# Attention: upper-half value matmuls four steps earlier, query projections five to six steps later

## The reference

```python
q = (x @ Wq).reshape(b, n, 16, 64).transpose(0, 2, 1, 3) * scale
kv = concat([null_kv, x @ Wkv], axis=1)            # 1025 keys, one head of 64, shared
sim = einsum('bhid,bjd->bhij', q, kv)              # masked above the diagonal
attn = softmax(sim)
out = einsum('bhij,bjd->bhid', attn, kv)           # keys are also the values
return out.transpose(0, 2, 1, 3).reshape(b, n, 1024) @ Wout
```

## Time and profile before

| | |
|---|---|
| median of 3 runs | 1478.52 us (1477.1 to 1479.38) |
| the profiled execution | 1478.79 us, span 1477.1 us |
| attention, first score tile of pair 0 to that of pair 15 | 450.70 to 1006.75 us of the span |
| TensorE / VectorE / ScalarE / GpSimd busy over the span | 86% / 77% / 62% / 23% |
| mean granted TensorE clock | 0.956 |
| DMA engines | 59 GB/s mean, 24.9% of their time |

### The profile page before, as it was taken

The page is one execution under the profiler, slowest core; times in us unless marked ns, Lnnn a source line. Parts: engine busy times, 40 slices in busy tenths (PEclk is TensorE's granted clock), DMA queues, the critical chain, the costliest instruction groups (busy, mean ns, idle before and its releaser), DMA issues. The chain is left out here.

```text
span 1477.1 us, 28019 instructions
## 1 busy us (share of the span) xinstructions
PE 1271.0 (86%) x8305; PEld 535.3 (36%) x8368; DVE 1136.6 (77%) x1941; ACT 919.3 (62%) x1915; POOL 332.7 (23%) x552
## 2 busy tenths in 40 slices
PE   3699999999757999999989999999967999999985
PEld 2122222222234555555556555555641222222222
DVE  6889999999856666676644666666649999999996
ACT  3288888888726555555533555555334888888884
POOL 4200000001003334333422333343331000000200
PEclk9599999999969999999999999999976999999999
DMA  4512112452122222222220222220043211135412
GB/s 126 167 42 59 53 52 65 76 94 62 30 53 45 46 46 45 44 44 45 45 45 6 49 50 49 49 56 12 1 128 98 59 49 51 48 79 87 83 44 58
DMA packets 58909, 86.49 MB, mean 59 GB/s; under 512 B 22288, under 2 KB 32464, under 8 KB 58832
## 3 DMA queue, kind: packets, MB, share of 16 engines
q1 hardware_dynamic: 58832, 85.53, 24.9%
HBM read 37.79 MB, written 22.54 MB: 41 GB/s over the span
## 5 line engine op out<-in xcount | busy, mean ns | idle before, releaser
L916 DVE TENSOR_REDUCE neg_max<-ps 128x1 f32<-128x1024 f32 x512 | 601.5, 1218 | 53.2 <-PE ps L1157 44.0
L771 ACT ACTIVATE arena<-ps 128x512 f32<-128x512 f32 x1024 | 538.8, 603 | 150.3 <-PE ps L1172 147.5
L1172 PE MATMUL ps<-arena 50*128 50x512 bf16 x1024 | 311.1, 388 | 59.8 <-ACT arena L771 41.4
L992 DVE TENSOR_REDUCE a_neg_max<-ps 128x1 f32<-128x129 f32 (+7 forms) x256 | 193.2, 755 | 168.7 <-PE ps L1274 165.3
L1157 PE MATMUL ps<-arena 48*128 48x512 bf16 x1024 | 269.2, 397 | 18.9 <-DVE neg_max L916 16.9
L1186 PE MATMUL ps<-arena 128*32 128x512 f32 x2048 | 275.5, 611 | 3.3
L578 POOL TENSOR_SCALAR arena<-arena,a_rsum 128x128 f32<-128x128 f32 (+7 forms) x256 | 191.3, 747 | 376.8 <-DVE a_rsum L1000 365.7
L1274 PE MATMUL ps<-arena 128*128 128x512 bf16 (+4 forms) x1281 | 227.8, 301 | 15.2 <-ACT null_out L722 4.8
L685 ACT ACTIVATE arena<-ps,a_neg_max 128x129 f32<-128x129 f32 (+7 forms) x256 | 189.5, 741 | 60.7 <-DVE a_neg_max L992 58.5
L1172 PEld LDWEIGHTS ps<-arena 50*128 50x128 bf16 x1024 | 77.5, 94 | 413.2 <-ACT arena L771 370.8
L695 ACT ACTIVATE arena<-ps 128x128 f32<-128x128 f32 (+1 forms) x192 | 87.0, 453 | 206.6 <-PE ps L1287 205.3
(11 more groups left out here) (120 smaller groups left out, 804.5 us busy)
## 6 DMA issues: line engine op xcount, KB each, us to landing
arena<-stack_dram SPq DMA_DIRECT2D x128, 192.0 KB, 3.4
stack_dram<-arena SPq DMA_DIRECT2D x48, 256.0 KB, 3.7
arena<-arena SPq DMA_DIRECT2D x32, 384.0 KB, 4.4
o_dram<-arena SPq DMA_DIRECT2D x32, 256.0 KB, 2.1
arena<-arena SPq DMA_DIRECT2D x32, 256.0 KB, 5.0
arena<-o_dram SPq DMA_DIRECT2D x30, 256.0 KB, 4.4
arena<-max_dram SPq DMA_DIRECT2D x256, 1.0 KB
arena<-arena SPq DMA_DIRECT2D x32, 128.0 KB, 4.8
```

Of the source, the lines that this page charges most:

```text
L771: nc.scalar.activation(probs[:, t, :], ps[:, EXP_BANK[t], :], ACT.Exp, scale=F_SCALE).then_inc(probs_ready, 1)
L916: nc.vector.tensor_reduce(neg_max[:, g, t:t + 1], ps[:, bank:bank + 2, :].rearrange("p a b -> p (a b)"), AX, ALU.max, negate=True).then_in ...
L992: nc.vector.tensor_reduce(a_neg_max[:, t:t + 1], ps[:, S_BANK[t % 2]:S_BANK[t % 2] + (n + HALF - 1) // HALF, :].rearrange("p a b -> p (a b ...
L1172: ins = nc.tensor.matmul(ps[:, bank, :], stack[rows, g, 1, kt * P:(kt + 1) * P], stack[rows, g, 0, h * HALF:(h + 1) * HALF], start=True, s ...
```

## The change

Three constants change, and three calls change places so that the order of the uses of bank 7 stays that of the steps. The value matmuls of the upper half (V1, four parts) go from steps 8 to 11 to steps 4 to 7. The two query halves go from steps 3 and 6 to steps 9 and 11. All that hangs on the two tables moves along: on VectorE the output copy of V1 from step 12 to step 8 and `q_rests` from steps 4 and 7 to 10 and 12; on ScalarE `q_first` and `q_second` to steps 10 and 12; on GpSimd `q_third` behind `normalize` of steps 9 and 11; and with it the moment at which SyncE issues its transfers. No instruction is added or removed.

```diff
         V0_STEPS = (0, 1)
-        Q_STEPS = (3, 6)
-        V1_STEPS = (8, 9, 10, 11)
+        V1_STEPS = (4, 5, 6, 7)
+        Q_STEPS = (9, 11)
...
-            return (2 if first else 4 * pg + 1) + h
+            return (2 if first else 4 * pg + 2) + h
...
+                            if t - 1 == V1_STEPS[-1] and not (first and k == 0):
+                                o_evac(pg - 1, before[1], 1)
                             if t - 1 in Q_STEPS and not (last and k == 1):
                                 q_rests(pg + 1, Q_STEPS.index(t - 1))
-                            if t - 1 == V1_STEPS[-1] and not (first and k == 0):
-                                o_evac(pg - 1, before[1], 1)
...
+                            if t in V1_STEPS and not (first and k == 0):
+                                a_values(pg - 1, bb, 1, 4 * pg + 1, V1_STEPS.index(t))
                             if t in Q_STEPS and not no_q:
                                 h = Q_STEPS.index(t)
                                 queries(pg + 1, q_uses(pg, first and k == 0, h), bn, (k + 1) % 2, h)
-                            if t in V1_STEPS and not (first and k == 0):
-                                a_values(pg - 1, bb, 1, 4 * pg + (1 if no_q else 3), V1_STEPS.index(t))
```

## The result

| | before | changed |
|---|---|---|
| median | 1478.5 us | 1634.8 us (1632.98 to 1636.15) |
| ratio to before | | 1.1057, 95% interval 1.1038 to 1.1076 |
| span of the profiled execution | 1477.1 us | 1631.3 us |
| TensorE busy | 1271.0 us (86%) | 1301.4 us (80%) |
| mean granted TensorE clock | 0.956 | 0.924 |

What follows compares the result with a forecast made beforehand. TensorE was taken to bound the attention (busy 28.18 of 30 us). A steady pair of 46.8 instead of 35.6 us gave +134 over twelve pairs, +158 in all; from 1478.8 us this made 1637 us, range 1590 to 1670.

Steps and rivals of the forecast that it cites:

- The light half: Steps 0 to 7 of a steady pair, now with V1: 18.3 us, plus 2.8 us for the low clock.
- The walk through the heavy half: Steps 8 to 15, from tile 8: query halves start at 3.0 and 7.8 us, TensorE done at 16.8, `q_third` at 16.4.
- The load: SyncE's six query transfers after the second `q_third`: unchanged, landing 9.3 us later, so the next pair's first tile stalls 8.9 us.
- The queueing behind `normalize` of step 11: On GpSimd the second `q_third` stands behind `normalize`, which needs a late VectorE reciprocal: `normalize` 13.8 to 14.9, `q_third` 15.2 to 16.4.
- Rival 3: At pair starts the load isn't waited for, only work order counts: 1466 us, or no change; chance 0.03 (0.02 faster).
- Rival 4: The second half's `q_third` or landings come later still: 1.5 to 3 us more a pair, 1660 to 1680 us; chance 0.10.
- The clock: After each stall at a pair's start TensorE runs at half clock for 5.6 us, costing 2.8 us.
- Rival 1: Clock loss after the stalls at pair starts is small or none: 39 us less, 1598 us; chance 0.12.
- Rival 2: SyncE's six query transfers take 6.2 us instead of 9.3: 43 us less, 1594 us; chance 0.04.
- Rival 3's other half: Without a load wait, VectorE paces a heavy half of 16.8 us: pair 35.9 us, no change; chance 0.01.
- Pair 8: The pair with 22 us of output matmuls after its queries: light half +6.8, heavy half -3.1, together +3.7 us.
- Pair 15: The pair without queries: light half 18.3 + 2.8 against 13.1, heavy half 16.2 against 20.5, together +3.7 us.

## Why the prediction was right

1637 us was forecast, 1634.8 measured, and the path is the one described. By its steps:

- **The light half** was put at 18.3 + 2.8 = 21.1 us; it took 20.8 (pair 3). With fillers in the stall, and so without the low clock, it took 592.64 - 574.34 = 18.3.
- **The walk through the heavy half.** First projection at 3.0 us after tile 8: measured 3.3 (601.80 - 598.50). Second at 7.8: 8.4. TensorE done at 16.8: about 17.7. Second third done at 16.4: 17.2 (615.72). The order of waits was right at each place, the 0.8 and 0.4 us before the projections too (0.87 and 0.51); the walk ran 0.6 to 0.9 us short behind tile 10. These slips put the third and TensorE's end late alike, so the stall hardly felt them.
- **The load** was put at 9.3 us; from the second third to the next pair's tile it took 9.6. The stall of 8.9 us was 9.1.
- **The queueing behind `normalize` of step 11** is shown: with the third ahead of it 2.8 us a pair are gone, and moved alone into the kernel before, the third makes 141 of the 156 us. Rival 3, that the load isn't waited for, falls already by the 127.5 us of DMA waits. Rival 4, that the split ends later, is there in small: the third came 0.8 us later than said, not 1.5 to 3.
- **The clock** was put at 2.8 us a stall, 39 in all; taking it away gave 34, or 34.1 / 14 = 2.4 us a stall. Rival 1, little or no clock loss, falls. The lower figure that the Trainium skill's worked case gives (TensorE: Matmul & The Clock Gate, HAM oscillation; 0.83 us for each wait) would have been too small here.
- **Rival 2**, a shorter load, falls for this kernel: landings are about as before (L414 4.4 to 5.4 us, median 4.9). The Trainium skill's rule of 2.0 us plus bytes at 436 GB/s (DMA: Bandwidth & Descriptors, Anatomy of one DMA) is a fit for single transfers of GpSimd's path. The estimate of 5.6 us by it isn't reached by this load of six transfers from SyncE, which took 9.6.
- **Rival 3's other half**, that levelling wins nothing as VectorE's chain then sets the pace, is borne out in part. With V1 at 7 to 10 tile 13 waits 0.63 us for an exponential, and with V1 at 4 to 7 behind early queries three tiles of the heavy half wait 1.7 us in all; but bank 7 costs time in these kernels too, and no run has levelled halves without it.

Sizes that were off, in both directions: a steady pair gained 11.5 to 11.7 us where 11.2 was said; pair 0 +8.7 for +6.9 (its light half took 8.9 us for 8.1, the way to the landing 25.7 for 24.7); pair 9 +9.9 for +9.2. Pair 8 was put at +3.7 and got 1.5 us shorter. Before, a low clock stretch fell into its output matmuls, as these rows of the kernel before show (16 matmuls each):

```profile
776.15 2.87 PE L1321 MATMUL ps<-wout,arena 128*128 128x128 f32 x16 [1.88 <-DVE x L1023]
...
779.67 3.78 PE L1321 MATMUL ps<-wout,arena 128*128 128x128 f32 x16
```

From start to start these two groups and the one matmul pair behind each take 3.5 and 4.4 us; at full clock each takes 2.4. That is 3.2 of the 5.2 us by which pair 8 missed. After, with the same wait ahead of them, they ran at full clock:

```profile
864.22 2.05 PE L1321 MATMUL ps<-wout,arena 128*128 128x128 f32 x16 [1.88 <-DVE x L1023]
```

Pair 15 was put at +3.7 and took +1.2: its light half took 19.6 us for 21.1, since the low clock ended 3 us after the work began, and its heavy half saved 1 us more than said. The total is nearer than its parts: +157.4 for the attention against +158 said is partly luck, since the steady pairs' excess and the shortfall of pairs 8 and 15 cancel.

## What to carry to other kernels

Before work is moved within a loop, follow what it produces: here the projection's product goes through ScalarE, VectorE, GpSimd and a load, 17 us from the second projection's start in the kernel before, and the next iteration's first instruction waits for it. The slack of that path (7 us here) is the budget of the move, and a single instruction queued behind another one that waits can spend it alone. When a shared PSUM bank changes hands, count the handover through the other engines (1.5 to 2 us here) before placing users one step apart; moving one projection by one step the other way, so that the bank was free in time, gave 0.8%, of which a good half is shown to be its own.

## What the runs showed of the hardware that I had not expected

- The granted clock fell to half without any long stall. With waits of 1.54, 1.90 and 1.49 us in successive steps, or 2.13 and 1.75 us, the next matmuls ran at half speed (3.55 us for eight that take 1.94). With fillers in the gaps it stayed up. The same wait of 1.88 us ahead of the output matmuls was followed by a low stretch in one kernel and by none in the other, so a given wait doesn't settle it.
- Filler matmuls, useless in themselves, brought 34 us (1634.8 to 1600.7) by keeping the clock up through a stall that they didn't shorten.
- The same transfer L412 took 0.48 us to issue on SyncE when none of the six was under way (615.84) and 1.26 us with three others of the six under way (618.29). Six transfers of half the size were issued in 0.6 us each where the full ones took up to 1.8, and that was 1.3 us of the load's length (3.2 instead of 4.5 us from first to last issue).
